# Experts stage: two buffers for the split activations, and VectorE and GpSimd exchange halves of the low second weights

## The chip, the cores and the metric

The kernel runs on one core of one Trainium2 chip. The metric is the device time of one execution in microseconds (us), given as the median of several runs. Five engines work side by side: TensorE (PE, whose weight loads the profile lists apart as PEld), VectorE (DVE), ScalarE (ACT), GpSimd (POOL) and SyncE (SP, which here only issues DMAs). They share the on-chip memory SBUF and wait for one another with semaphores. TensorE writes into PSUM.

## The reference, cut to what matters

The program is a chain of four blocks over 32 sequences of 112 rows of 256 features: cross attention, self attention with a mixture of experts behind it, a second cross attention, and a linear layer on quantised values. The change lies in the mixture of experts alone:

```python
gate_logits = nx @ gate_W
topk_vals, topk_idx = jax.lax.top_k(gate_logits, TOP_K)          # 2 of 8 experts
for e in range(N_EXPERTS):
    h = jax.nn.gelu(jnp.einsum('bsd,fd->bsf', nx, fc1_w[e]) + fc1_b[e], approximate=False)
    y = jnp.einsum('bsf,df->bsd', h, fc2_w[e]) + fc2_b[e]        # 1024 features -> 256
    moe_out = moe_out + y * dense_gates[..., e:e + 1]
```

## The kernel before

The rows that chose an expert lie in DRAM sorted by expert (`slots`), and `experts` works through them in 63 tiles of 128 rows (`MOE_TILES`), each of one expert. All second weights (`mem["w2"]`) lie in SBUF; the first weights of a tile (1 MB) come by DMA, two tiles ahead.

For a tile t there are two products. The first gives 1024 hidden features (`hidden`, L1428, 32 matmuls), to which ScalarE applies the Gelu (`act_T`, L1336, eight instructions). The second product, y, is made at the speed of rounded numbers (type fp32r) and with nearly the precision of float32: each operand is split into a rounded part and what the rounding left over, and three products are summed, high x high, high x low and low x high (L1447 and L1448, 8 chunks of 128 features, 3 matmuls each, 24 in all). Each split part has one buffer of its own, used by all tiles in turn:

- `w2H`, the rounded second weights, by ScalarE in two halves of 1024 elements (`weights_high`, L1328; counted by `w2_high`, two a tile). The first half belongs to the chunks 0 to 3, the second to 4 to 7.
- `aH`, the rounded activations, by ScalarE (L1343, `a_high`).
- `aL`, the low activations, `act_T` minus `aH`, by VectorE (L1399, `a_low`).
- `w2L`, the low second weights, `w2` minus `w2H`: the first half by GpSimd (L1359, `w2_low`), the second by VectorE (L1401, `w2_low_late`).

Every engine has its own instruction queue and runs the same loop (`over_tiles`). In step t:

- TensorE: the hidden product of tile t, the two transposes that prepare the rows of tile t + 1 (L1436), then y of tile t - 1. Before y it waits for `a_high`, `a_low` and `w2_low`; ahead of chunk 4 it also waits for `w2_low_late`. After chunk 3 it raises `y_half`, after chunk 7 `y_mm`.
- ScalarE: the Gelu of tile t; after `y_half` (y of tile t - 1 has read its first half) the first half of `w2H`; after `y_mm` (y of tile t - 1 is done) `aH` and then the second half of `w2H`.
- VectorE: the copies of the transposed rows of tile t + 1 (L1386), then y of tile t - 1 out of PSUM with its bias (L1394, after `y_mm`), a load of tile t's expert number into a register (L1397), `aL`, and the second half of `w2L`.
- GpSimd: a load of the expert number (L1357) and the first half of `w2L`, as soon as the first half of `w2H` is there. It has nothing else in this stage.

When the stage ends, the next stage's instructions stand behind it in each queue, GpSimd's casts and subtractions of `cross_last` (L1579 to L1599) among them.

Of the kernel before, what the change touches and what calls it, by code (L numbers as in the profile page):

```python
# [13 lines left out]
F32R = mybir.dt.float32r  # L14
BF16 = mybir.dt.bfloat16
U32 = mybir.dt.uint32
ALU = mybir.AluOpType
ACT = mybir.ActivationFunctionType
# [630 lines left out]
def self_attention(nc, mem, w, residual):  # L649
# [3 lines left out]
    with ExitStack() as ctx:  # L653
# [43 lines left out]
        tiles, ends, spare = sb("tiles", [1, NE]), sb("ends", [1, NE]), sb("spare", [1, NE])  # L697
        past, skipped = (wqkv[0:1, i, 0:(MOE_TILES + 1) * NE].rearrange("p (t e) -> p t e", e=NE) for i in range(2))
        tile_at = sb("tile_at", [1, MOE_TILES + 1])
        held, held_dve = sb("held", [1, 4]), sb("held_dve", [1, 2])  # L700
        weights_in, cleared, wo_in = sem("weights_in"), sem("cleared"), sem("wo_in")
        nT_mm, nT_ready = sem("nT_mm"), sem("nT_ready")
        q_mm, q_whole, q_ready, q_rounded = sem("q_mm"), sem("q_whole"), sem("q_ready"), sem("q_rounded")
# [526 lines left out]
def experts(nc, mem, w, residual):  # L1230


    with ExitStack() as ctx:
# [10 lines left out]
        wf, mx = sb("wf", [128, 2 * D]), {n: sb(f"mx_{n}", [128, 2 * D]) for n in ("t", "magic", "q", "d")}  # L1244
        mx.update((n, sb(f"mx_{n}", [128, 2 * D // MX])) for n in ("scale", "inv"))
        lent = lambda n, rows, size: nc.alloc_sbuf_tensor_at(f"e_{n}", [128, size * D], F32R, offset=mem["lent_at"] + rows * D * 4)
        w2H, w2L, aH, aL = lent("w2H", 0, 8), lent("w2L", 8, 8), lent("aH", 16, 4), lent("aL", 20, 4)
        w2_high, w2_low, w2_low_late, a_high, a_low, y_half = (sem(n) for n in ("w2_high", "w2_low", "w2_low_late", "a_high", "a_low", "y_half"))
        mx_step, w_ready = sem("mx_step"), sem("w_ready")
        NCH = HID // 128  # L1250
# [15 lines left out]
        def emit(block):  # L1266
# [53 lines left out]
            @block.scalar  # L1320
            def _(act):
                act.wait_ge(mem["fc1_b_in"], 16)
                act.wait_ge(mem["routed"], 1)
                act.wait_ge(mem["w2_in"], 16 * NE)
                act.wait_ge(mem["saved"], 16 * (NB - LENT))

                def weights_high(e, half):
                    act.activation(w2H[:, half * HALF:(half + 1) * HALF], weights_half(e, half), ACT.Copy).then_inc(w2_high, 1)  # L1328

                def step(t, par):  # L1330
                    if exists(t, MOE_TILES):
                        e = act.value_load(mem["tile_expert"][0:1, bass.ds(t, 1)], min_val=0, max_val=NE - 1)
                        act.wait_ge(h_mm, t + 1)
                        wait(act, a_low, t - 1)
                        for c in range(NCH):
                            last = act.activation(act_T[par][:, c * TILE:(c + 1) * TILE], hidden[par][:, c // 4, (c % 4) * TILE:(c % 4 + 1) * TILE],  # L1336
                                                  ACT.Gelu, bias=b1[:, bass.ds(e, 1), c:c + 1].rearrange("p a c -> p (a c)"))
                        last.then_inc(h_ready, 1)
                        wait(act, y_half, t)
                        weights_high(e, 0)  # L1340
                        act.wait_ge(h_ready, t + 1)
                        wait(act, y_mm, t)
                        act.activation(aH[:, :], act_T[par], ACT.Copy).then_inc(a_high, 1)  # L1343
                        weights_high(e, 1)
                    if isinstance(t, int) and t == 1:
                        mem["round_weights"](act)

                over_tiles(act, step)

            @block.gpsimd  # L1350
            def _(pool):
                pool.wait_ge(mem["routed"], 1)
                pool.wait_ge(mem["w2_in"], 16 * NE)

                def step(t, par):
                    if exists(t, MOE_TILES):
                        e = pool.value_load(mem["tile_expert"][0:1, bass.ds(t, 1)], min_val=0, max_val=NE - 1)  # L1357
                        pool.wait_ge(w2_high, 2 * t + 1)
                        pool.tensor_tensor(w2L[:, 0:HALF], weights_half(e, 0), w2H[:, 0:HALF], ALU.subtract).then_inc(w2_low, 1)  # L1359

                over_tiles(pool, step)

            @block.vector
            def _(dve):
# [12 lines left out]
                def step(t, par):  # L1377
# [18 lines left out]
                    if exists(t, MOE_TILES):  # L1396
                        e = dve.value_load(mem["tile_expert"][0:1, bass.ds(t, 1)], min_val=0, max_val=NE - 1)  # L1397
                        dve.wait_ge(a_high, t + 1)
                        dve.tensor_tensor(aL[:, :], act_T[par], aH[:, :], ALU.subtract).then_inc(a_low, 1)  # L1399
                        dve.wait_ge(w2_high, 2 * t + 2)  # L1400
                        dve.tensor_tensor(w2L[:, HALF:2 * HALF], weights_half(e, 1), w2H[:, HALF:2 * HALF], ALU.subtract).then_inc(w2_low_late, 1)  # L1401
                    if isinstance(t, int) and t == MOE_TILES - 1:
                        dve.wait_ge(bias_in, 32)
                        for action in quantise[:EARLY]:
# [9 lines left out]
            def _(pe):  # L1414
# [5 lines left out]
                def step(t, par):  # L1420
# [17 lines left out]
                    if exists(t - 1, MOE_TILES):  # L1438
# [4 lines left out]
                        for c in range(NCH):  # L1443
                            rows, cols = slice(c * TILE, (c + 1) * TILE), slice(c * D, (c + 1) * D)
                            if c == quarter:
                                pe.wait_ge(w2_low_late, t)
                            for i, (left, right) in enumerate(((aH, w2H), (aH, w2L), (aL, w2H))):  # L1447
                                last = pe.matmul(y_ps[:, 0:D], left[:, rows], right[:, cols], start=(c == 0 and i == 0), stop=(c == NCH - 1 and i == 2))  # L1448
                            if c == quarter - 1:
                                last.then_inc(y_half, 1)  # L1450
# [699 lines left out]
def program(nc, names, args, out):  # L2150
    w = dict(zip(names, args))
    ctx_t = w["ctx_t"]
    with ExitStack() as ctx:
# [18 lines left out]
        mem["saved"], mem["returned"] = sem("saved"), sem("returned")  # L2172
        mem["kept_rows"] = nc.dram_tensor("kept_rows", [T, NB - LENT, D], F32, kind="Internal").ap()
        mem["rates"], mem["shifts"], mem["rates_ready"] = sb("rates", [T, NB, 2]), sb("shifts", [T, NB, 2]), sem("rates_ready")
        first = cross_first(nc, mem, ctx_t, w, residual)
        with ExitStack() as weights:
            for name, shape in (("room", [128, ROOM]), ("w1", [128, 2, 2, HID]), ("w2", [128, NE, HID // 128, D])):
# [53 lines left out]
```

## Time and profile before

| | us |
|---|---|
| median of 3 runs (1979.08 to 1984.09) | 1982.87 |
| the profiled execution | 1980.91 |
| its span, first to last instruction | 1978.8 |
| the experts' y products, first to last start (trace) | 863.11 to 1290.37 |

Shares of the span: TensorE 95% busy, its weight loads 83%, VectorE 76%, ScalarE 64%, GpSimd 56%. TensorE's mean granted clock is 0.975 of full speed.

The page gives the busy time of each engine, the span in slices, the chain of work that ended last, and groups of instructions by line with what ended the idle time before them. Matmuls overlap, so a busy TensorE is not one at its peak; a weight load's row (PEld) shows by its start where a matmul began. A stage is read best from the timeline of each engine, in order of time.

### The profile page before, as it was taken

To read this page: it belongs to the slowest core of one execution; us is meant where nothing else is said; L and a number is where in the kernel's file an instruction comes from. 1 tells how busy PE (TensorE), PEld (TensorE's weight loads), DVE (VectorE), ACT (ScalarE), POOL (GpSimd) and SP (SyncE) were. 2 spreads that over 40 slices of the span, in tenths; PEclk is the share of its full clock that TensorE was granted. 3 is DMA by queue.
4 is the path that set the end of the run, shared out by engine and by line. 5 is a ranking of instruction groups with operands and counts; after the bars stand their busy time and mean duration, and the time that the engine had idled before them with its cause. 6 is when DMAs were issued, how large, how long until landed. Compare 5 with 4: busy or idle time off the path is not lost.

```text
span 1978.8 us, 61792 instructions
## 1 busy us (share of the span) xinstructions
PE 1877.6 (95%) x20887; PEld 1642.6 (83%) x20887; DVE 1498.3 (76%) x3375; ACT 1264.7 (64%) x2720; POOL 1098.7 (56%) x1680
## 2 busy tenths in 40 slices
PE   7999999999699999889999999959999999999996
PEld 5888888888578888689999999958888888888895
DVE  6788878877378888656666666666888888888886
ACT  2555555555377777557777777737767777777773
POOL 4565556555157676623333333377676767676751
PEclk9999999999799999899999999969999999999998
DMA  8222322331051111175555555421111111111100
GB/s 235 89 87 88 115 87 87 98 108 30 1 181 32 37 37 39 61 259 185 187 191 200 191 185 187 157 78 59 36 33 42 33 41 30 40 34 40 34 15 10
DMA packets 116596, 182.05 MB, mean 92 GB/s; under 512 B 10851, under 2 KB 94563, under 8 KB 116067
## 3 DMA queue, kind: packets, MB, share of 16 engines
q1 hardware_dynamic: 110386, 166.51, 26.2%
q0 software_dynamic: 6144, 14.69, 2.5%
q8 instruction: 40, 0.66, 0.1%
q14 instruction: 26, 0.21, 0.0%
HBM read 127.68 MB, written 53.48 MB: 92 GB/s over the span
## 4 chain that ended last, share of the span: by engine, by line
PE 52%; DVE 2%; issue 1%; POOL 1%; ACT 1%; DMA 0%; ACTq 0%; POOLq 0%; DVEq 0%
PE ps_quad L1428 11%; PE ps_out L1448 9%; PE ps_quad L182 6%; PE ps_quad L102 4%; PE ps_out L114 4%; PE ps_turned L108 4%; PE ps_quad L1879 3%; PE ps_proj L1899 3%; PE ps_turned L182 3%; PE ps_proj L182 2%; PE ps_proj L1904 1%; PE ps_proj L1436 1%; DVE c_negmax L119 1%; ACT c_probs L134 0%; PE ps_quad L1894 0%
## 5 line engine op out<-in xcount | busy, mean ns | idle before, releaser
L1359 POOL TENSOR_TENSOR e_w2L<-w,e_w2H 128x1024 fp32r<-128x1024 f32 x63 | 149.2, 2369 | 294.1 <-ACT e_w2H L1328 294.1
L1428 PE MATMUL ps_quad<-e_xT,w 128*128 128x128 f32 x2016 | 235.9, 275 | 1.7 <-DVE e_xT L1386 1.7
L1428 PEld LDWEIGHTS ps_quad<-e_xT,w 128*128 128x128 f32 x2016 | 231.1, 192 | 2.2 <-DVE e_xT L1386 2.2
L364 ACT ACTIVATE a_probsT<-ps_quad 125x1792 f32<-125x1792 f32 x96 | 159.8, 1665 | 101.6 <-PE ps_quad L533 101.6
L1336 ACT ACTIVATE e_act_T<-ps_quad,fc_b 128x128 f32<-128x128 f32 x504 | 137.0, 383 | 97.9 <-PE ps_quad L1428 97.7
L134 ACT ACTIVATE c_probs<-ps_quad,c_negmax 112x375 f32<-112x375 f32 x256 | 143.6, 571 | 66.2 <-DVE c_negmax L119 66.2
L1399 DVE TENSOR_TENSOR e_aL<-e_act_T,e_aH 128x1024 fp32r<-128x1024 f32 x63 | 151.8, 2409 | 37.9 <-ACT e_aH L1343 37.9
L1448 PE MATMUL ps_out<-e_w2H,e_aH 128*128 128x256 f32 x504 | 148.8, 295 | 13.3 <-DVE e_aL L1399 7.1
L126 DVE TENSOR_SCALAR c_probs<-c_probs,c_recip 112x375 f32<-112x375 f32 x256 | 150.9, 630 | 4.6
L421 DVE TENSOR_REDUCE a_negmax<-ps_turned 112x2 f32<-112x750 f32 x128 | 120.1, 938 | 34.1 <-PE ps_turned L519 33.9
L119 DVE TENSOR_REDUCE c_negmax<-ps_quad 112x2 f32<-112x750 f32 x128 | 114.0, 930 | 41.4 <-PE ps_quad L102 40.9
L1448 PE MATMUL ps_out<-e_w2H,e_aL 128*128 128x256 f32 x504 | 143.8, 285 | 0.0
L1448 PE MATMUL ps_out<-e_w2L,e_aH 128*128 128x256 f32 x504 | 143.7, 285 | 0.0
L419 DVE TENSOR_REDUCE a_negmax<-ps_quad 112x4 f32<-112x1500 f32 x64 | 110.2, 1721 | 36.5 <-PE ps_quad L519 36.5
L1328 ACT ACTIVATE e_w2H<-w 128x1024 fp32r x126 | 134.9, 1071 | 1.7 <-PE ps_out L1448 1.7
L1448 PEld LDWEIGHTS ps_out<-e_w2H,e_aH 128*128 128x128 f32 x504 | 97.3, 193 | 20.3 <-issue 18.9
L1394 DVE TENSOR_TENSOR e_y<-ps_out,e_b 128x256 f32<-128x256 f32 x63 | 26.8, 425 | 110.0 <-PE ps_out L1448 110.0
L108 PEld LDWEIGHTS ps_turned<-ident,c_probs 112*125 112x125 f32 x768 | 100.8, 188 | 7.6 <-issue 2.4
L108 PE MATMUL ps_turned<-ident,c_probs 112*125 112x112 f32 x768 | 103.8, 271 | 1.8 <-ACT c_probsT L130 1.8
L130 ACT ACTIVATE c_probsT<-ps_turned 125x672 f32<-125x672 f32 x128 | 95.1, 743 | 10.7 <-PE ps_turned L108 8.2
L359 ACT ACTIVATE a_kT<-ps_proj,a_bk 128x376 f32<-128x376 f32 x64 | 36.7, 574 | 101.0 <-PE ps_proj L182 101.0
L1448 PEld LDWEIGHTS ps_out<-e_w2H,e_aL 128*128 128x128 f32 x504 | 97.6, 194 | 0.0
(352 smaller groups left out, 6012.4 us busy)
## 6 DMA issues: line engine op xcount, KB each, us to landing
w<-in_fc_t SPq DMA_DIRECT2D x71, 1024.0 KB, 4.9
slots<-a_zeros SPq DMA_DIRECT2D x60, 512.0 KB, 4.9
a_cT<-in_ctx_t SPq DMA_DIRECT2D x32, 375.0 KB, 3.5
c_cT<-in_ctx_t SPq DMA_DIRECT2D x32, 375.0 KB, 3.2
e_xg<-slots SPq DMA_DIRECT2D x63, 128.0 KB, 3.9
slots<-e_y SPq DMA_DIRECT2D x63, 128.0 KB, 1.7
out<-c_fo SPq DMA_DIRECT2D x32, 112.0 KB, 1.9
residual<-in_x SPq DMA_DIRECT2D x1, 2912.0 KB, 19.0
```

The source lines that it names most:

```text
L108: last = pe.transpose(self.turned[:, j, c * T:(c + 1) * T], self.probs[u][:, j, c * self.chunk:(c + 1) * self.chunk], ident[0:T, 0:T])
L119: dve.tensor_reduce(self.negmax[:, u, :], self.scores[u % 2], AX, ALU.max, negate=True).then_inc(self.max_ready, 1)
L126: last = dve.tensor_scalar(p, p, self.recip[:, u, j:j + 1], None, ALU.mult)
L134: last = act.activation(self.probs[u][:, j, :], self.scores[u % 2][:, j, :], ACT.Exp, bias=self.negmax[:, u, j:j + 1], accum_out=self.sums ...
L182: last = pe.matmul(dst, left, right, start=(i == 0), stop=(i == len(terms) - 1))
L364: act.activation(probsT[:, 2 * i:2 * i + 2, :, :].rearrange("p c r x -> p r c x"), quad[0:KC, :, 0:2 * HALF].rearrange("p r (c x) -> p r c ...
L1328: act.activation(w2H[:, half * HALF:(half + 1) * HALF], weights_half(e, half), ACT.Copy).then_inc(w2_high, 1)
L1336: last = act.activation(act_T[par][:, c * TILE:(c + 1) * TILE], hidden[par][:, c // 4, (c % 4) * TILE:(c % 4 + 1) * TILE], ACT.Gelu, bias= ...
L1359: pool.tensor_tensor(w2L[:, 0:HALF], weights_half(e, 0), w2H[:, 0:HALF], ALU.subtract).then_inc(w2_low, 1)
L1399: dve.tensor_tensor(aL[:, :], act_T[par], aH[:, :], ALU.subtract).then_inc(a_low, 1)
L1428: last = pe.matmul(hidden[par][:, c // 4, (c % 4) * TILE:(c % 4 + 1) * TILE], mem["w1"][:, par, k, c * 128:(c + 1) * 128], xT[par][:, k, : ...
L1448: last = pe.matmul(y_ps[:, 0:D], left[:, rows], right[:, cols], start=(c == 0 and i == 0), stop=(c == NCH - 1 and i == 2))
```

## The change

`aH` and `aL` get a second buffer each, by the tile's parity. ScalarE rounds the activations right after the Gelu (it waits for its own `h_ready` and for y of tile t - 2), ahead of both halves of `w2H`, where the rounding stood between them and waited for y of tile t - 1. VectorE and GpSimd exchange the halves of `w2L`: VectorE makes the first half after `aL`, as soon as the first half of `w2H` is there; GpSimd makes the second, after the second half of `w2H`. The semaphores go with the halves: `w2_low` is now VectorE's, `w2_low_late` GpSimd's. Two small tiles (`held`, `held_dve`) are allocated in another place.

```diff
-        w2H, w2L, aH, aL = lent("w2H", 0, 8), lent("w2L", 8, 8), lent("aH", 16, 4), lent("aL", 20, 4)
+        w2H, w2L = lent("w2H", 0, 8), lent("w2L", 8, 8)
+        aH = [lent("aH0", 16, 4), ctx.enter_context(nc.sbuf_tensor("e_aH1", [128, HID], F32R))]
+        aL = [lent("aL0", 20, 4), ctx.enter_context(nc.sbuf_tensor("e_aL1", [128, HID], F32R))]
...
                         last.then_inc(h_ready, 1)
+                        act.wait_ge(h_ready, t + 1)
+                        wait(act, y_mm, t - 1)
+                        act.activation(aH[par][:, :], act_T[par], ACT.Copy).then_inc(a_high, 1)
                         wait(act, y_half, t)
                         weights_high(e, 0)
-                        act.wait_ge(h_ready, t + 1)
                         wait(act, y_mm, t)
-                        act.activation(aH[:, :], act_T[par], ACT.Copy).then_inc(a_high, 1)
                         weights_high(e, 1)
...
-                        pool.wait_ge(w2_high, 2 * t + 1)
-                        pool.tensor_tensor(w2L[:, 0:HALF], weights_half(e, 0), w2H[:, 0:HALF], ALU.subtract).then_inc(w2_low, 1)
+                        pool.wait_ge(w2_high, 2 * t + 2)
+                        pool.tensor_tensor(w2L[:, HALF:2 * HALF], weights_half(e, 1), w2H[:, HALF:2 * HALF], ALU.subtract).then_inc(w2_low_late, 1)
...
                         dve.wait_ge(a_high, t + 1)
-                        dve.tensor_tensor(aL[:, :], act_T[par], aH[:, :], ALU.subtract).then_inc(a_low, 1)
-                        dve.wait_ge(w2_high, 2 * t + 2)
-                        dve.tensor_tensor(w2L[:, HALF:2 * HALF], weights_half(e, 1), w2H[:, HALF:2 * HALF], ALU.subtract).then_inc(w2_low_late, 1)
+                        dve.tensor_tensor(aL[par][:, :], act_T[par], aH[par][:, :], ALU.subtract).then_inc(a_low, 1)
+                        dve.wait_ge(w2_high, 2 * t + 1)
+                        dve.tensor_tensor(w2L[:, 0:HALF], weights_half(e, 0), w2H[:, 0:HALF], ALU.subtract).then_inc(w2_low, 1)
...
-                            for i, (left, right) in enumerate(((aH, w2H), (aH, w2L), (aL, w2H))):
+                            for i, (left, right) in enumerate(((aH[1 - par], w2H), (aH[1 - par], w2L), (aL[1 - par], w2H))):
```

## Rows read from the trace of the kernel before

**Rows 1.** The page, busy us, share of the span, instructions.

```profile
PE 1877.6 (95%) x20887; PEld 1642.6 (83%) x20887; DVE 1498.3 (76%) x3375; ACT 1264.7 (64%) x2720; POOL 1098.7 (56%) x1680
```

**Rows 2.** Busy us per engine by stretch, then granted clock, DMA share, GB/s.

```profile
863.11:1290.37 427.26, 418.13 (x3560) 411.58 (x3560) 285.08 (x309) 315.61 (x679) 147.96 (x66) 1.00 0.56 191
```

**Rows 3.** Timeline, PEld: start us, us, instruction [idle before, releaser].

```profile
1043.21 0.19 PEld L1448 LDWEIGHTS ps_out<-e_w2H,e_aH 128*128 128x128 f32 x1 [0.38 <-issue]
...
1046.07 3.66 PEld L1428 LDWEIGHTS ps_quad<-e_xT,w 128*128 128x128 f32 x32
1049.65 0.25 PEld L1436 LDWEIGHTS ps_proj<-ident,e_xg 128*128 128x128 f32 x2
1049.87 0.19 PEld L1448 LDWEIGHTS ps_out<-e_w2H,e_aH 128*128 128x128 f32 x1
```

**Rows 4.** Timeline, GpSimd and VectorE in the same tile.

```profile
1046.28 2.38 POOL L1359 TENSOR_TENSOR e_w2L<-w,e_w2H 128x1024 fp32r<-128x1024 f32 x1 [4.22 <-ACT e_w2H L1328]
...
1046.60 0.42 DVE L1394 TENSOR_TENSOR e_y<-ps_out,e_b 128x256 f32<-128x256 f32 x1 [1.68 <-PE ps_out L1448]
1047.55 2.19 DVE L1399 TENSOR_TENSOR e_aL<-e_act_T,e_aH 128x1024 fp32r<-128x1024 f32 x1 [0.53 <-ACT e_aH L1343]
```

**Rows 5.** Lines L1399 and L1401, duration ns min/median/max of 63.

```profile
L1399 DVE TENSOR_TENSOR e_aL<-e_act_T,e_aH x63: 1224/2602/2652, 860.4 to 1287.7; 128x1024 fp32r<-128x1024 f32 x63
...
L1401 DVE TENSOR_TENSOR e_w2L<-w,e_w2H x63: 1210/1212/3333, 863.0 to 1290.2; 128x1024 fp32r<-128x1024 f32 x63
```

**Rows 6.** Timeline, ScalarE, one tile.

```profile
1042.98 2.17 ACT L1336 ACTIVATE e_act_T<-ps_quad,fc_b 128x128 f32<-128x128 f32 x8 [1.58 <-PE ps_quad L1428]
1045.04 1.06 ACT L1328 ACTIVATE e_w2H<-w 128x1024 fp32r x1
1046.45 1.06 ACT L1343 ACTIVATE e_aH<-e_act_T 128x1024 fp32r<-128x1024 f32 x1 [0.35 <-PE ps_out L1448]
1047.42 1.04 ACT L1328 ACTIVATE e_w2H<-w 128x1024 fp32r x1
```

**Rows 7.** Line L1397, VectorE's sequencer, duration ns min/median/max.

```profile
L1397 DVEq TENSOR_LOAD <-tile_expert x63: 300/308/544, 855.2 to 1286.6; - x63
```

**Rows 8.** Timeline, GpSimd and VectorE at the end of the stage.

```profile
1289.37 0.98 POOL L1579 TENSOR_TENSOR c_held<-minus_half 1x1 f32<-1x1 f32 x1
...
1291.20 1.28 POOL L1597 TENSOR_TENSOR c_wkL<-c_wk,c_wkH 128x512 fp32r<-128x512 f32 x1
1292.55 2.14 POOL L1599 TENSOR_TENSOR c_wkH<-c_wk,c_wkH 64x512 fp32r<-64x512 f32 x1
...
1287.67 2.63 DVE L1399 TENSOR_TENSOR e_aL<-e_act_T,e_aH 128x1024 fp32r<-128x1024 f32 x1 [0.64 <-ACT e_aH L1343]
1290.23 3.33 DVE L1401 TENSOR_TENSOR e_w2L<-w,e_w2H 128x1024 fp32r<-128x1024 f32 x1
```

**Rows 9.** Busy us per engine by stretch; the third number from the right is the clock.

```profile
861.10:863.10 2.00, 0.00 (x0) 0.00 (x0) 2.00 (x2) 2.00 (x9) 0.85 (x1) 1.00 0.75 240
863.10:864.50 1.40, 1.36 (x11) 1.39 (x12) 1.40 (x3) 0.27 (x2) 0.00 (x0) 1.00 1.00 367
864.50:867.90 3.40, 3.40 (x18) 3.40 (x17) 0.57 (x2) 1.36 (x2) 1.61 (x1) 0.50 1.04 392
...
499.30:506.10 6.80, 6.52 (x70) 4.87 (x70) 1.04 (x6) 2.35 (x4) 2.15 (x6) 0.50 0.00 0
...
1341.00:1345.00 4.00, 4.00 (x40) 3.64 (x42) 2.41 (x4) 3.25 (x8) 3.88 (x7) 1.00 0.17 23
```

**Rows 10.** Timeline, PEld and PE, where they had stalled.

```profile
863.11 0.19 PEld L1448 LDWEIGHTS ps_out<-e_w2H,e_aH 128*128 128x128 f32 x1 [3.37 <-issue]
867.08 4.07 PEld L1428 LDWEIGHTS ps_quad<-e_xT,w 128*128 128x128 f32 x32
...
498.82 0.41 PE L548 MATMUL ps_turned<-ident,a_negmax 112*128 112x112 f32 x2 [1.21 <-DVE a_negmax L419]
...
1340.92 0.33 PE L1879 MATMUL ps_quad<-c_xT,c_wq 128*128 128x112 f32 x1 [1.00 <-ACT c_probs L134]
```

More of the change, by code:

```diff
@@ L699, in self_attention @@
         tile_at = sb("tile_at", [1, MOE_TILES + 1])
-        held, held_dve = sb("held", [1, 4]), sb("held_dve", [1, 2])
+        held, held_dve = mem["held"], mem["held_dve"]
         weights_in, cleared, wo_in = sem("weights_in"), sem("cleared"), sem("wo_in")
@@ L2174, in program @@
         mem["rates"], mem["shifts"], mem["rates_ready"] = sb("rates", [T, NB, 2]), sb("shifts", [T, NB, 2]), sem("rates_ready")
+        mem["held"], mem["held_dve"] = sb("held", [1, 4]), sb("held_dve", [1, 2])
         first = cross_first(nc, mem, ctx_t, w, residual)
```

## The prediction

> **What bounds the kernel now.** I read the page's shares first: TensorE is busy 95% of the span and no other engine over 76% [rows 1]. Only the experts stage is touched, so the next view is the stretch from the first start of the y products to the last: 427.26 us, TensorE busy 418.13, clock 1.00 [rows 2]. Those are 62 periods of 6.89 us. The timeline of weight loads shows a period's parts: y from 1043.21 to 1046.07 is 2.86, the hidden product and two transposes up to the next y at 1049.87 are 3.80, together 6.66 [rows 3]. What is over, 0.38, is an idle wait in front of y, in every second tile. All the change can give is thus 62 x (6.89 - 6.66) = 14 us.
>
> What ends that wait? VectorE's aL. It takes 1.22 at the least, but 2.60 in the median [rows 5]. The timeline says why: GpSimd's subtraction runs from 1046.28 to 1048.66, aL is issued at 1047.55 and ends at 1049.74, 1.08 after GpSimd has ended [rows 4]. It does nearly all its work after GpSimd, whenever it was issued. So two subtractions on these two engines, both from SBUF to SBUF, do not run side by side here. VectorE's copy of y out of PSUM, issued inside the same GpSimd instruction, took its 0.42 [rows 4]; it isn't held.
>
> At the end of the stage the same thing is seen the other way round [rows 8]. GpSimd's one-element operation, issued at 1289.37, ends at 1290.35, just after aL (1290.30). VectorE's second half of w2L was issued at 1290.23, seven hundredths before aL ended. Yet GpSimd goes first, and the half takes 3.33, to 1293.56, that is 1.09 after GpSimd's subtraction of 1291.20 to 1292.48. The next GpSimd subtraction, issued at 1292.55, ends at 1294.69, 1.13 after VectorE: it waited, and only some 0.15 of the 1.28 that the one before it took was hidden in that wait. So each engine waits for the other's whole instruction, and a waiting GpSimd goes before the next VectorE instruction, even one that follows at once.
>
> The Trainium skill's page "SBUF — State Buffer", section "SBUF: two separate sides", states such a rule: VectorE instructions with two SBUF inputs and GpSimd's share a port pair, which the first to start holds for its whole instruction while the other is fully blocked. If the held GpSimd subtraction then ran its whole 2.37, and not 0.14 less as the row has it, each period below would be 0.14 longer, 9 us in all. The trace agrees with the lock and puts the hidden start-up at 0.15.
>
> **The change, part by part.** Times are from the first weight load of y of tile t - 1, for a tile without idle time. ScalarE: the Gelu starts at 0.15 (1042.98 is 0.23 ahead of 1043.21, less the idle 0.38) and ends at 2.3 [rows 3, 6]. aH follows at 2.35, where it stood at 3.24; the new buffer is what allows it, since y of tile t - 2 is long done. Consecutive copies start 0.97 apart [rows 6]: w2H's first half at 3.3 to 4.4, its second at 4.3 to 5.35 (it may not start before 3.24). ScalarE's work is the same, done before the next Gelu at 6.8. GpSimd, 0.18 behind the copy it waits for (1046.10 to 1046.28), is issued at 5.5, where it was issued at 3.07.
>
> VectorE: it must first copy y out, at 3.39 (1046.60 - 1043.21). Then comes the register load of 0.31 with its bookkeeping [rows 7]. No row shows how soon aL could follow, since aH always came later; it lies between 0.42 (the copy's own time) and 0.95 (1046.60 to 1047.55) [rows 4]. I take 0.8, since the load and three more sequencer steps have to pass. aL then runs at 4.2 to 5.4 unhindered (1.22), and w2L's first half at 5.35 to 6.55 (1.21) [rows 5]. y of tile t could start at 6.66: this half is just in time.
>
> But VectorE now holds the memory from 4.2 to 6.55, and GpSimd asks at 5.5. It runs from 6.55 and ends at 6.55 + 2.37 - 0.14 = 8.8. TensorE needs the second half four chunks into y, at 6.66 + 1.43 = 8.1. It stalls 0.7 in the middle of y. That stall delays the end of y, hence VectorE's copy and aL by 0.7 (aL at 4.9 to 6.1 of the next tile), but not GpSimd's request: it still comes at 5.5, now inside aL. By rows 8 GpSimd then goes before the first half of w2L, for which TensorE waits at the start of y.
>
> From there the order keeps itself. Counted from the end of a y product (E): copy at 0.53, aL 1.33 to 2.55. ScalarE waited for the same end and runs w2H's second half at 0.38 to 1.42 [rows 6]; GpSimd asks at 1.60, inside aL again. GpSimd 2.55 to 4.78, w2L's first half until 4.78 + 1.08 = 5.86, y at 5.94. TensorE was ready at 3.80, so it idles 2.14 in front of every y. The period is 2.86 + 5.94 = 8.8 in place of 6.89: 62 x 1.91 = 118 us. If aL came 0.3 later, GpSimd would go ahead of it and the period would be 9.1; if 0.3 earlier, 8.5. So +99 to +137 before the clock.
>
> **The clock.** Stalls of 3.37 and of 1.21 were each followed by a fall of the granted clock from 1.00 to 0.50 (2.4 to 1.2 GHz); after one of 1.00 it stayed [rows 9, 10]. A stall of 2.14 lies between two that fell, so I take it to fall. At 863 it fell 1.4 after TensorE had resumed, at 498.8 it fell 0.5 after, and the first low stretch lasted 3.4 us: y then took 867.08 - 863.11 = 3.97, 1.11 more than 2.86 [rows 10]. Had that stretch lain wholly in y, y would have lost up to half of it, some 1.5. The price per tile lies between 0 and 1.5; I take 1.4, as a shorter stall lets the fall come sooner, like the one at 498.8. A slow stretch under the hidden product costs nothing, since 2.14 of slack cover it. 62 x 1.4 = 87 us.
>
> Sum: 118 + 87 = 205, on the profiled execution's 1980.9 (span 1978.8; the median of 1982.87 is 0.1% above it): 2186 us.
>
> At nothing I cost: the moved small tiles; SyncE's DMAs, as none is moved and a longer period leaves them more time; VectorE's copy of the transposed rows, now queued behind the late half, which ends 0.1 before y starts and so leaves it y's 2.86 for its 0.72. Behind GpSimd's later wait nothing of this stage is queued. Behind ScalarE's new wait stand the two copies, but it is met. The first and last tile may add or take 3 us; not counted.
>
> **Rivals.**
> 1. The same order, but the clock stays at 1.00: 1980.9 + 118 = 2099. For it: the stall of 1.00 without a fall. Against it: a fall after 1.21.
> 2. VectorE keeps the memory for both of its instructions whenever GpSimd's request falls into aL. Then only the stall in the middle of y is left, 0.7 to 0.8 a tile: period 7.4, 62 x 0.5 = 32, 2013 us. Against it: the same pair of instructions at 1290.23 let GpSimd in between.
> 3. The other side, faster: GpSimd's second half meets its date. It is in time if it ends by 8.1, so if it gets the memory by 5.9; that needs VectorE's two subtractions to be over by then, 0.65 earlier than I have it, or not to hold GpSimd's at all. From that point on TensorE's period is 6.66: minus 14 us, 1967. For it: rows 4 show this pair with only VectorE waiting; no row has a 128x1024 GpSimd subtraction held. Against it: 1292.55 in rows 8, which was.
>
> **How the numbers follow.** Forecast 0.63 (own range 2160 to 2210), rival 1 0.18, rival 2 0.05, rival 3 0.09, no change 0.03, slower in another way 0.02. The range must take in the forecast and rival 1 with the bounds of aL's start (2099 - 19 = 2080): 2080 to 2210, which leaves out 0.19. A measurement tells this kernel from no change at about 0.3%, 6 us: faster 0.09, same 0.03, slower 0.88.
>
> **What would show it.** In the profile after: aL at about 1.22 in nearly all tiles; VectorE's half of w2L at 3.3, in place of 1.21; GpSimd's subtraction at some 3.2 (0.95 of waiting), in place of 2.37; TensorE idle some 2.1 in front of y with VectorE's w2L as what ended it; a clock well under 1.00 from 870 to 1290. aL still long with GpSimd's unhindered at 2.37 would be wrong order; a period of 7.4 with the idle time in front of chunk 4 would be rival 2; GpSimd and VectorE side by side at 2.37 and 1.21 with no idle TensorE, rival 3.

## The result and the profile after

The changed kernel takes 2183.61 us in the median of four runs (2176.62 to 2184.95), against 1983.48 for the kernel before: ratio 1.1012 (95% interval 1.0991 to 1.1032). It is 10% slower. The profiled execution took 2182.3 us, with a span of 2180.2. Where executions of an experiment came with a mean clock of 0.65 to 0.84 (four in all, of experiments 7 and 8), they are left out of its ratio and its bounds.

The page, busy us and shares of the span, and the chain of work that ended last. They answer to [rows 1]: TensorE is listed as more busy than before, 1962.5 in place of 1877.6, with the same 20887 instructions, so its instructions have become longer. VectorE's subtraction of `w2L` is now 10% of the chain.

```profile
PE 1962.5 (90%) x20887; PEld 1721.2 (79%) x20887; DVE 1558.0 (71%) x3375; ACT 1283.7 (59%) x2720; POOL 1145.0 (53%) x1680
...
PE ps_out L1451 12%; DVE e_w2L L1404 10%; PE ps_quad L182 6%; PE ps_quad L102 4%; PE ps_out L114 3%; PE ps_turned L108 3%; PE ps_quad L1882 3%; PE ps_turned L182 3%; PE ps_proj L1902 3%; PE ps_proj L182 2%; ACT e_w2H L1330 2%; PE ps_proj L1907 1%; DVEq L1400 1%; DVE c_negmax L119 1%; ACT c_probs L134 0%
```

Busy time by stretch, from the first start of the y products to the last, in the columns of [rows 2]. Then one y product that ran at full clock, and the next, which did not.

```profile
865.32:1495.40 630.08, 500.94 (x3560) 487.89 (x3560) 347.14 (x309) 334.17 (x683) 196.40 (x67) 0.86 0.38 130
1045.56:1048.41 2.85, 2.82 (x23) 2.85 (x24) 0.42 (x2) 2.16 (x3) 0.00 (x0) 1.00 0.90 355
...
1054.45:1058.46 4.01, 3.98 (x23) 4.01 (x24) 0.41 (x2) 2.32 (x3) 0.00 (x0) 0.65 0.66 263
```

The stretch is 630.08 in place of 427.26, 202.8 more; the span grew by 201.4. So the whole loss lies here. A period is 630.08 / 62 = 10.16 in place of 6.89, and the clock is 0.86 in place of 1.00.

Instructions that write `aL` and `w2L`, duration ns min/median/max, as in [rows 5].

```profile
L1402 DVE TENSOR_TENSOR e_aL<-e_act_T,e_aH x63: 1224/1225/1227, 862.8 to 1490.7; 128x1024 fp32r<-128x1024 f32 x63
...
L1404 DVE TENSOR_TENSOR e_w2L<-w,e_w2H x63: 1218/3400/3424, 864.0 to 1491.8; 128x1024 fp32r<-128x1024 f32 x63
L1362 POOL TENSOR_TENSOR e_w2L<-w,e_w2H x63: 2565/3112/3191, 864.9 to 1491.2; 128x1024 fp32r<-128x1024 f32 x63
```

`aL`, which had been held (2602 in the median), now never is. VectorE's half of `w2L`, which had been free (1212), is held in nearly every tile, and GpSimd's subtraction has 0.75 of waiting in it (3112 against 2367 before).

Timelines of ScalarE, GpSimd, VectorE and the weight loads, one tile, to be read beside [rows 3, 4, 6].

```profile
1048.82 1.06 ACT L1330 ACTIVATE e_w2H<-w 128x1024 fp32r x1 [0.37 <-PE ps_out L1451]
...
1050.06 3.08 POOL L1362 TENSOR_TENSOR e_w2L<-w,e_w2H 128x1024 fp32r<-128x1024 f32 x1 [5.80 <-ACT e_w2H L1330]
...
1048.94 0.42 DVE L1397 TENSOR_TENSOR e_y<-ps_out,e_b 128x256 f32<-128x256 f32 x1 [2.96 <-PE ps_out L1451]
1049.69 1.22 DVE L1402 TENSOR_TENSOR e_aL<-e_act_T,e_aH 128x1024 fp32r<-128x1024 f32 x1 [0.33 <-issue]
1050.83 3.39 DVE L1404 TENSOR_TENSOR e_w2L<-w,e_w2H 128x1024 fp32r<-128x1024 f32 x1
...
1045.56 0.19 PEld L1451 LDWEIGHTS ps_out<-e_w2H,e_aH 128*128 128x128 f32 x1 [2.27 <-issue]
1048.41 3.66 PEld L1431 LDWEIGHTS ps_quad<-e_xT,w 128*128 128x128 f32 x32
1051.99 0.25 PEld L1439 LDWEIGHTS ps_proj<-ident,e_xg 128*128 128x128 f32 x2
1054.45 0.19 PEld L1451 LDWEIGHTS ps_out<-e_w2H,e_aH 128*128 128x128 f32 x1 [2.21 <-issue]
```

Read it from the end of y, 1048.41. GpSimd asks 1.65 later, in the middle of `aL` (1049.69 to 1050.91), and is let in when `aL` ends, although VectorE's half is issued at 1050.83. GpSimd ends at 1053.14, VectorE's half 1.08 after that, at 1054.22, and y starts 0.23 later. TensorE, ready at 1052.24, has idled 2.21.

The first three y products, weight loads:

```profile
865.32 0.19 PEld L1451 LDWEIGHTS ps_out<-e_w2H,e_aH 128*128 128x128 f32 x1 [2.33 <-issue]
867.52 0.19 PEld L1451 LDWEIGHTS ps_out<-e_w2H,e_aH 128*128 128x128 f32 x1 [0.71 <-POOL e_w2L L1362]
...
874.80 0.19 PEld L1451 LDWEIGHTS ps_out<-e_w2H,e_aH 128*128 128x128 f32 x1 [2.03 <-issue]
```

The first y stalls 0.71 ahead of chunk 4, on GpSimd. That delays its end, and from the second y on the stall is in front of y and about 2 us long.

### The profile page after: what moved, and what is told of

Read it like the earlier page. It is cut to its first block, busy times and chain, and to the rows that moved or that the text cites. A ratio compares the mean times of both kernels' runs of the same rounds, so it can differ in the third digit from the quotient of the medians.

```text
span 2180.2 us, 61791 instructions
## 1 busy us (share of the span) xinstructions
PE 1962.5 (90%) x20887; PEld 1721.2 (79%) x20887; DVE 1558.0 (71%) x3375; ACT 1283.7 (59%) x2720; POOL 1145.0 (53%) x1680
## 4 chain that ended last, share of the span: by engine, by line
PE 40%; DVE 11%; issue 5%; ACT 2%; DVEq 1%; POOL 1%; ACTq 0%; DMA 0%; POOLq 0%
PE ps_out L1451 12%; DVE e_w2L L1404 10%; PE ps_quad L182 6%; PE ps_quad L102 4%; PE ps_out L114 3%; PE ps_turned L108 3%; PE ps_quad L1882 3%; PE ps_turned L182 3%; PE ps_proj L1902 3%; PE ps_proj L182 2%; ACT e_w2H L1330 2%; PE ps_proj L1907 1%; DVEq L1400 1%; DVE c_negmax L119 1%; ACT c_probs L134 0%
## 5 line engine op out<-in xcount | busy, mean ns | idle before, releaser
L1362 POOL TENSOR_TENSOR e_w2L<-w,e_w2H 128x1024 fp32r<-128x1024 f32 x63 | 195.6, 3105 | 449.5 <-ACT e_w2H L1330 449.5
L1451 PE MATMUL ps_out<-e_w2H,e_aH 128*128 128x256 f32 x504 | 183.1, 363 | 131.3 <-DVE e_w2L L1404 130.8
L1451 PEld LDWEIGHTS ps_out<-e_w2H,e_aH 128*128 128x128 f32 x504 | 132.1, 262 | 144.5 <-issue 143.8
L1397 DVE TENSOR_TENSOR e_y<-ps_out,e_b 128x256 f32<-128x256 f32 x63 | 26.7, 425 | 263.4 <-PE ps_out L1451 263.4
L1404 DVE TENSOR_TENSOR e_w2L<-w,e_w2H 128x1024 fp32r<-128x1024 f32 x63 | 212.0, 3366 | 0.0
L1451 PE MATMUL ps_out<-e_w2H,e_aL 128*128 128x256 f32 x504 | 178.9, 355 | 0.0
L1451 PE MATMUL ps_out<-e_w2L,e_aH 128*128 128x256 f32 x504 | 178.4, 354 | 0.0
L1451 PEld LDWEIGHTS ps_out<-e_w2H,e_aL 128*128 128x128 f32 x504 | 134.1, 266 | 0.0
L1451 PEld LDWEIGHTS ps_out<-e_w2L,e_aH 128*128 128x128 f32 x504 | 133.7, 265 | 0.0
```

The source lines that it names most:

```text
L1362: pool.tensor_tensor(w2L[:, HALF:2 * HALF], weights_half(e, 1), w2H[:, HALF:2 * HALF], ALU.subtract).then_inc(w2_low_late, 1)
L1404: dve.tensor_tensor(w2L[:, 0:HALF], weights_half(e, 0), w2H[:, 0:HALF], ALU.subtract).then_inc(w2_low, 1)
```

## The experiments

**Theory.** Two subtractions on VectorE and GpSimd, both with all their inputs in SBUF, exclude each other for whole instructions (the lock). The time goes to the order in which the two engines get it (about 120 us), and to the clock, which falls after the stalls this order makes (about 85 us). **Rivals.** The lock is no part of it, and VectorE or GpSimd simply has too much to do; the second buffers, not the exchange, cost the time; the clock would have fallen anyway.

**1. No GpSimd: VectorE makes both halves.**

```diff
-                        pool.tensor_tensor(w2L[:, HALF:2 * HALF], ...).then_inc(w2_low_late, 1)
+                        dve.wait_ge(w2_high, 2 * t + 2)
+                        dve.tensor_tensor(w2L[:, HALF:2 * HALF], ...).then_inc(w2_low_late, 1)
```

> Both halves of the low second weights on VectorE (first half, then second half right behind it), GpSimd does nothing in the experts stage; the two buffers stay. Theory (VectorE's and GpSimd's subtractions hold the memory against each other for whole instructions): with GpSimd silent no subtraction on VectorE takes more than 1.22; counted from the start of a y product aL ends at 5.4, the first half at 6.55, the second at 7.7, and TensorE needs them at 6.66 and 8.1; period 6.66 to 6.7, clock 1.00, 1980.9 - 14 = 1967 us (1962 to 1971), faster than both kernels. Rival (it is the early rounding with its new order on VectorE, or simply too much low work late in the tile, that stalls TensorE): VectorE has 1.21 more to do in each tile, and the kernel stays at 2184 or gets slower.

Measured: 1974.88 us, ratio 0.9963 (0.995 to 0.9976). Taking work away from GpSimd and giving all of it to VectorE makes the changed kernel 209 us faster: VectorE doesn't have too much to do. (That GpSimd doesn't either, experiment 2 shows.) The gain over the kernel before is 8 us, less than expected, and only 0.4 of it lies between the first and the last y product (426.83 in place of 427.26); the rest lies ahead of them and behind. VectorE's timeline, GpSimd's and the weight loads show why:

```profile
895.03 1.57 DVE L1400 TENSOR_TENSOR e_aL<-e_act_T,e_aH 128x1024 fp32r<-128x1024 f32 x1 [0.34 <-issue]
896.52 2.29 DVE L1402 TENSOR_TENSOR e_w2L<-w,e_w2H 128x1024 fp32r<-128x1024 f32 x1
...
895.49 2.25 POOL L1600 TENSOR_TENSOR c_wkL<-c_wk,c_wkH 128x512 fp32r<-128x512 f32 x1
...
1047.61 1.22 DVE L1400 TENSOR_TENSOR e_aL<-e_act_T,e_aH 128x1024 fp32r<-128x1024 f32 x1 [0.32 <-issue]
...
1054.51 1.22 DVE L1400 TENSOR_TENSOR e_aL<-e_act_T,e_aH 128x1024 fp32r<-128x1024 f32 x1 [0.54 <-issue]
1055.65 1.22 DVE L1402 TENSOR_TENSOR e_w2L<-w,e_w2H 128x1024 fp32r<-128x1024 f32 x1
...
1057.09 0.19 PEld L1451 LDWEIGHTS ps_out<-e_w2H,e_aH 128*128 128x128 f32 x1 [0.24 <-issue]
```

In every second tile VectorE waits 0.54 and not 0.32 ahead of `aL`, its first half ends at 1056.87, and y follows 0.22 later, after 0.24 of idle time. And GpSimd isn't silent: with nothing left to do in this stage it makes the next stage's subtractions already from 895 on, and the lock stretches three of VectorE's halves to 2.3, with idle times of 1.46 and 1.32 in front of y.

**2. GpSimd is made to wait for VectorE's half.**

```diff
+                        pool.wait_ge(w2_low, t + 1)
                         pool.wait_ge(w2_high, 2 * t + 2)
```

> The changed kernel with one wait more: GpSimd starts its half only when VectorE's half of the same tile is done. Nothing is taken away. Theory (the loss comes from the order GpSimd before VectorE's second subtraction): VectorE's half falls from 3.38 to 1.21 and y starts without idle time; GpSimd runs 2.37 from 6.65 to 9.0 and TensorE stalls 0.9 in front of chunk 4, which needs it at 8.1; period 7.4 to 7.6, and as a stall of 1.00 did not lower the clock before, the clock stays near 1.00: 1980.9 + 62 x 0.6 = 2018 us (2010 to 2030). Rival (GpSimd's lateness alone is the cause): the wait makes GpSimd later still, so 2184 us or more.

Measured: 2037.73 us, ratio 1.0276 (1.0259 to 1.0294). The instructions that write `w2L`, and the weight load of chunk 4:

```profile
L1405 DVE TENSOR_TENSOR e_w2L<-w,e_w2H x63: 1215/1218/1221, 864.7 to 1348.3; 128x1024 fp32r<-128x1024 f32 x63
L1363 POOL TENSOR_TENSOR e_w2L<-w,e_w2H x63: 2386/2397/2415, 866.2 to 1349.7; 128x1024 fp32r<-128x1024 f32 x63
...
1047.87 0.19 PEld L1452 LDWEIGHTS ps_out<-e_w2H,e_aH 128*128 128x128 f32 x1 [1.01 <-POOL e_w2L L1363]
```

The same work on the same engines in the other order, with one wait more, is 146 us faster. Both subtractions run at their free length, and the stall has moved in front of chunk 4 and is 1.01; the period is 7.80 and the clock of the stretch 1.00. The order was the cause, not the amount.

**3. VectorE's half reads its first input from PSUM.**

```diff
-  dve.tensor_tensor(w2L[:, 0:HALF], weights_half(e, 0), w2H[:, 0:HALF], ALU.subtract)
+  dve.tensor_tensor(w2L[:, 0:HALF], hidden[par].rearrange("p a f -> p (a f)"), w2H[:, 0:HALF], ALU.subtract)
```

> The changed kernel, but VectorE's half of the low second weights takes its first input from PSUM (the tile's hidden features, the same 128x1024 float32) where it took the weights from SBUF; so the low first half is not the weights' remainder, and the output is not the reference's. Same engines, sizes, order and waits. Theory (what is held is the memory access of a VectorE instruction with two SBUF inputs): this instruction takes about 1.2 also while GpSimd runs; GpSimd, asking at 5.5 after aL's end at 5.4, takes 2.37 and is done at 7.9, before 8.1; period 6.7, no idle time, about 1967 us (1960 to 1975). Rival (the two engines keep each other from running whatever the memory, or share it by bandwidth): still 3.4 for the half, 2184 us.

Measured: 1972.5 us, ratio 0.9953 (0.9938 to 0.9969). The same two lines:

```profile
L1404 DVE TENSOR_TENSOR e_w2L<-ps_quad,e_w2H x63: 1214/1217/1219, 858.8 to 1277.5; 128x1024 fp32r<-128x1024 f32 x63
L1362 POOL TENSOR_TENSOR e_w2L<-w,e_w2H x63: 2383/2409/3119, 859.8 to 1277.9; 128x1024 fp32r<-128x1024 f32 x63
```

With GpSimd's operation, its place and its waits as in the changed kernel, one input of VectorE's taken from elsewhere gives back all of the 200 us and 11 more. Near 1042 the half is issued at 1042.32 and GpSimd's subtraction at 1042.46, and both run at their free length side by side. So the exclusion needs both of VectorE's inputs in SBUF. The Trainium skill's page "SBUF — State Buffer", section "SBUF: two separate sides", names a VectorE operation with two SBUF inputs as one that takes the pair of ports shared with GpSimd. The run agrees: with one input in PSUM, 1.217 beside 2.409. The half made here isn't that of the weights, so this run prices the lock and is no remedy.

**4. The stall is filled.** Eleven transposes whose result nobody reads stand before each y on TensorE; no other engine waits for them.

```diff
+                    if exists(t - 1, MOE_TILES):
+                        for i in range(FILL):          # FILL = 11
+                            pe.transpose(psum["turned"][:, 0, 0:128], ident[:, :], ident[:, :])
```

> The changed kernel with 11 transposes of the identity into an unused PSUM area ahead of each y product, about 11 x 0.164 = 1.8 us of TensorE work in the 2.0 us in which it idles. Theory (1.4 of the 3.3 us per tile are the granted clock, which falls after each stall): the clock stays at 1.00 and y takes 2.86, the waits behind VectorE's half stay; period 8.8, 2099 us (2090 to 2112), 85 us less than the changed kernel although TensorE does more. Rival (y is long for another reason, such as the memory's other readers): y stays at 4.0 to 4.3 and the time at 2184 us or more.

Measured: 2105.34 us, ratio 1.0617 (1.0599 to 1.0634). Stretch of the y products, and a y's first weight load:

```profile
860.29:1415.38 555.09, 496.18 (x4242) 483.00 (x4242) 349.08 (x309) 334.16 (x683) 198.83 (x67) 1.00 0.43 147
...
1048.70 0.19 PEld L1455 LDWEIGHTS ps_out<-e_w2H,e_aH 128*128 128x128 f32 x1 [1.04 <-issue]
```

TensorE has 682 instructions more in this stretch, and the kernel is 78 us faster: the idle time is cut to 1.04 (the eleven take 1.2 us, not the 1.8 reckoned) and the clock stays at 1.00. The period is 555.09 / 62 = 8.95. So the loss of the changed kernel splits into (8.95 - 6.89) x 62 = 128 us for the order and (10.16 - 8.95) x 62 = 75 us for the clock. The changed kernel's own periods at full clock, 8.89 from 1045.56 to 1054.45, give nearly the same split, 124 and 79.

**5. The buffers alone, halves as before; 6. the exchange alone, single buffers.**

```diff
 # 5: the changed kernel, but
+                        pool.tensor_tensor(w2L[:, 0:HALF], ...).then_inc(w2_low, 1)
+                        dve.tensor_tensor(w2L[:, HALF:2 * HALF], ...).then_inc(w2_low_late, 1)
 # 6: the kernel before, but
+                        pool.tensor_tensor(w2L[:, HALF:2 * HALF], ...).then_inc(w2_low_late, 1)
+                        dve.tensor_tensor(w2L[:, 0:HALF], ...).then_inc(w2_low, 1)
```

> Only the second buffers of the change: GpSimd keeps the first half of w2L and VectorE the second, as before. Theory (the lock, and a waiting GpSimd goes before VectorE's next instruction): the early aH moves w2H's first half to 3.3 to 4.4 after the start of y, so GpSimd asks at about 4.55, inside aL (4.2 to 5.4); it runs until some 7.65 and y starts about 1.0 late; VectorE's half after it is in time for chunk 4. After a late y, ScalarE is ahead, GpSimd asks at about 3.2 and the next y starts nearly on time, so the stalls alternate. Mean period 7.0 to 7.7 in place of 6.89: 1990 to 2035 us, slower than before, with the idle time in front of y ended by GpSimd. Rival (the exchange of the halves alone costs the time, buffers are harmless or help): 1965 to 1985 us. Second rival (the buffers cost all of it): 2150 us or more.

> Only the exchange of the halves: VectorE the first, GpSimd the second, with single buffers as before, so aH starts after the end of y. Counted from that end: aH 0.38 to 1.4, w2H's second half 1.35 to 2.4, GpSimd asks at 2.6; aL 1.47 to 2.69. Theory with GpSimd asking inside aL, by less than 0.1 us: GpSimd runs first, until 4.95, VectorE's half until 6.0, y starts at 6.1, TensorE idle 2.3 in front of y, period 8.96 and a falling clock: 2100 to 2210 us, as the whole change. Rival, aL ends before GpSimd asks: VectorE's half goes first, is over at 3.9, y starts nearly on time and the stall is in front of chunk 4, about 0.8 us with a period of 7.6 to 7.8: 2020 to 2040 us, like the kernel in which GpSimd was made to wait. Second rival (the exchange is harmless without the buffers): 1983 us.

Measured: the buffers alone 2011.1 us, ratio 1.0137 (1.0113 to 1.0162); the exchange alone 2188.65 us, ratio 1.1042 (1.1024 to 1.1061). The exchange by itself costs all of it; the buffers cost 30 us by themselves, in the alternation that was expected. GpSimd and the starts of y with the buffers alone:

```profile
1041.68 3.23 POOL L1362 TENSOR_TENSOR e_w2L<-w,e_w2H 128x1024 fp32r<-128x1024 f32 x1 [5.56 <-ACT e_w2H L1330]
1048.46 2.39 POOL L1362 TENSOR_TENSOR e_w2L<-w,e_w2H 128x1024 fp32r<-128x1024 f32 x1 [3.56 <-ACT e_w2H L1330]
...
1045.13 0.19 PEld L1451 LDWEIGHTS ps_out<-e_w2H,e_aH 128*128 128x128 f32 x1 [1.21 <-issue]
1052.01 0.19 PEld L1451 LDWEIGHTS ps_out<-e_w2H,e_aH 128*128 128x128 f32 x1 [0.19 <-issue]
```

With the exchange alone, VectorE and GpSimd:

```profile
1044.12 1.23 DVE L1399 TENSOR_TENSOR e_aL<-e_act_T,e_aH 128x1024 fp32r<-128x1024 f32 x1 [0.52 <-ACT e_aH L1343]
1045.27 3.38 DVE L1401 TENSOR_TENSOR e_w2L<-w,e_w2H 128x1024 fp32r<-128x1024 f32 x1
...
1045.22 2.35 POOL L1359 TENSOR_TENSOR e_w2L<-w,e_w2H 128x1024 fp32r<-128x1024 f32 x1 [8.22 <-ACT e_w2H L1328]
```

GpSimd asks at 1045.22, 0.13 before `aL` ends and 0.05 before VectorE's half is issued, and that is enough in all 63 tiles: VectorE's half takes 3.37 to 3.40 in each.

**7. Single buffers, all on VectorE; 8. two buffers, all on VectorE, and an early register load.** The first is the kernel before without GpSimd's half. The second is experiment 1 with:

```diff
+                        if exists(t, MOE_TILES):
+                            own = dve.value_load(mem["tile_expert"][0:1, bass.ds(t, 1)], ...)
                         dve.wait_ge(y_mm, t)
...
-                        e = dve.value_load(mem["tile_expert"][0:1, bass.ds(t, 1)], ...)
+                        e = own
                         dve.wait_ge(a_high, t + 1)
```

> The kernel before with GpSimd's half of w2L moved to VectorE, single buffers kept. Theory (what the kernel before loses in front of y is aL held by GpSimd; the buffers are worth next to nothing): aL 4.33 to 5.55 after the start of y, first half until 6.7, y at 6.75 to 6.8 in place of 6.66, second half until 7.85 against a need at 8.1. Period 6.75 to 6.8: 62 x 0.09 to 0.14 = 6 to 9 us less than before, 1974 to 1978 us, within 3 us of the kernel with all on VectorE and two buffers. Rival (the second buffers are what gains): 1983 us or more.

> The kernel with two buffers and all of w2L on VectorE, and VectorE's register load for the next tile ahead of the copy of y. In that kernel y waits 0.24 us in every second tile for VectorE's first half; aL follows the copy's start by 0.75 in one tile and 0.96 in the next. Theory (the load and its bookkeeping stand on the path): aL comes 0.33 to 0.54 earlier, the wait is gone, period 6.66 to 6.7, 62 x 0.12 = 7 us less than the 1974.9 us of that kernel: 1964 to 1970 us, faster than before by 0.6 to 1%. Rival (the wait is not VectorE's chain): 1975 us.

Measured: with single buffers 1985.9 us, ratio 1.0008 (0.9997 to 1.0018), no gain; with the early load 1965.35 to 1968.41 us, ratio 0.9919 (0.9902 to 0.9936). The first expectation was wrong by 8 to 12 us. VectorE's half and the weight load behind it, with single buffers:

```profile
1050.86 1.22 DVE L1399 TENSOR_TENSOR e_w2L<-w,e_w2H 128x1024 fp32r<-128x1024 f32 x1
...
1052.30 0.19 PEld L1448 LDWEIGHTS ps_out<-e_w2H,e_aH 128*128 128x128 f32 x1 [0.23 <-issue]
```

`aL` started where it was expected, 1.48 after the end of y, but y starts 0.22 after VectorE's half has ended, where 0.05 to 0.1 had been reckoned, and that in nearly every tile: period 6.92. The next stage's work on GpSimd, which experiment 1 showed, holds VectorE here too and costs some 3 us more. So with all on VectorE the two buffers are worth up to 11 us (1985.9 - 1974.9; the two profiled executions differ by 5.4), and the load 9 more.

**9. The changed kernel with the early load, twice.** The same edit as in 8, on the changed kernel; GpSimd keeps its half.

> The changed kernel, with VectorE's register load for the next tile moved ahead of the copy of y, so that aL follows the copy after about 0.42 us in place of 0.75 to 0.83. The prediction said that an aL that comes 0.3 earlier shortens the period by as much and leaves the order. Theory: the order keeps itself (GpSimd still asks inside aL), the period falls by 0.33 to 0.4 us, 62 times that is 20 to 25 us: about 2160 us if the clock falls as before, down to 2085 us if a stall of 1.8 us no longer lowers it. Rival: the order breaks, since aL is now over before GpSimd asks; then VectorE's half goes first and the stall in front of chunk 4 is left, 2010 to 2040 us. Second rival (the period is not set by VectorE's chain): 2183 us.

> The changed kernel with the early load once more, since it took 2077 to 2079 us in three executions and 1988 us in one at the same granted clock. Theory (two orders that keep themselves; which one a run falls into is settled by the first tiles): each execution is near 2077 or near 1988 us, none between; in the short one GpSimd's subtraction runs 2.4 and VectorE's half 1.22 in most tiles, in the long one 2.70 and 3.43. Rival (a disturbance of that one run): all near 2077 us, or scattered.

Measured: of 13 executions ten took 2076.8 to 2081.2 us and three 1982.3 to 1988.0, none between, all at a mean clock of 0.975 to 0.980. A profile of each, first of a long one, then of a short one (VectorE, GpSimd, weight loads):

```profile
1046.56 1.22 DVE L1404 TENSOR_TENSOR e_aL<-e_act_T,e_aH 128x1024 fp32r<-128x1024 f32 x1
1047.69 3.44 DVE L1406 TENSOR_TENSOR e_w2L<-w,e_w2H 128x1024 fp32r<-128x1024 f32 x1
...
1047.33 2.71 POOL L1362 TENSOR_TENSOR e_w2L<-w,e_w2H 128x1024 fp32r<-128x1024 f32 x1 [5.77 <-ACT e_w2H L1330]
...
1051.35 0.19 PEld L1453 LDWEIGHTS ps_out<-e_w2H,e_aH 128*128 128x128 f32 x1 [1.84 <-issue]
```

```profile
1045.54 1.22 DVE L1404 TENSOR_TENSOR e_aL<-e_act_T,e_aH 128x1024 fp32r<-128x1024 f32 x1
1046.67 1.22 DVE L1406 TENSOR_TENSOR e_w2L<-w,e_w2H 128x1024 fp32r<-128x1024 f32 x1
...
1047.13 3.04 POOL L1362 TENSOR_TENSOR e_w2L<-w,e_w2H 128x1024 fp32r<-128x1024 f32 x1 [3.91 <-ACT e_w2H L1330]
...
1050.22 0.19 PEld L1453 LDWEIGHTS ps_out<-e_w2H,e_aH 128*128 128x128 f32 x1 [0.27 <-POOL e_w2L L1362]
```

One program, two orders, and each keeps itself. In the long one y ends at 1045.69 and GpSimd asks 1.64 later, inside `aL`. In the short one y ends at 1044.67 and GpSimd asks 2.46 later, when `aL` is over and VectorE's half has begun; what is left is 0.27 ahead of chunk 4. ScalarE explains the two dates: where y starts late, its Gelu is long done and it waits only for the end of y; where y is on time, it still has the Gelu and two copies to do. What seems to have sent the profiled short run into its order is a row of ScalarE in the second tile, first of the short run, then of the long one, where the data were there:

```profile
872.42 1.06 ACT L1534 ACTIVATE c_wkH<-c_wk 128x1024 fp32r<-128x1024 f32 x1 [1.65 <-DMA c_wk<-in_L_xattn_Wk]
...
875.06 2.17 ACT L1338 ACTIVATE e_act_T<-ps_quad,fc_b 128x128 f32<-128x128 f32 x8 [0.24 <-issue]
```

```profile
868.69 1.04 ACT L1534 ACTIVATE c_wkH<-c_wk 128x1024 fp32r<-128x1024 f32 x1
```

The Gelu starts 5.76 after the end of the first y (869.30), in the long run 4.06 (867.32 to 871.38). A DMA that came late once kept ScalarE, hence GpSimd's next request, behind `aL`, and the order stayed for the 60 tiles left. This is read from one pair of traces, which also differ in the clock of the first y; no run delays that DMA alone. That it must be late enough, the changed kernel's trace suggests: there ScalarE waits 1.28 for the same data, in place of 1.65, and GpSimd's request (879.65) still falls inside `aL` (878.86 to 880.09). That the other short executions began in the same way isn't shown; they have no profile. The long order has one more thing to tell: its stalls of 1.84 leave the clock of the stage at 0.99 to 1.00, where those of 2.0 to 2.4 in the changed kernel go with 0.86, so the 0.4 to 0.5 us that `aL` comes earlier are worth 106 us.

**10. The kernel before with the Gelu's result in PSUM; 11. the same in the changed kernel.** The Gelu writes back into the `hidden` tile that it reads, and `aH` and `aL` take it from there.

```diff
-  last = act.activation(act_T[par][:, c * TILE:(c + 1) * TILE], hidden[par][:, c // 4, ...], ACT.Gelu, ...)
+  last = act.activation(hidden[par][:, c // 4, ...], hidden[par][:, c // 4, ...], ACT.Gelu, ...)
-  dve.tensor_tensor(aL[:, :], act_T[par], aH[:, :], ALU.subtract).then_inc(a_low, 1)
+  dve.tensor_tensor(aL[:, :], hidden[par].rearrange("p a f -> p (a f)"), aH[:, :], ALU.subtract).then_inc(a_low, 1)
```

> The kernel before, except that the Gelu writes its result back into the PSUM tile that it reads, and aH and aL take it from there. Theory (an instruction of VectorE with one input in PSUM is not held by GpSimd): aL takes 1.22 beside GpSimd's subtraction of 2.4, from about 4.35 to 5.6 after the start of y, and y starts at 6.66 without the 0.38 of idle time in every second tile: 1965 to 1972 us. Rival (the lock holds VectorE whatever its input): aL 2.6 as before, 1980 to 1986 us. Should the Gelu or the copy take longer on PSUM, ScalarE has about 1 us of slack in 6.66.

> The changed kernel, with the Gelu's result kept in PSUM, so that aL no longer shares anything with GpSimd. Theory: that does not save the change, since VectorE's first half is still held. Counted from the end of y: GpSimd asks at 1.65 and runs at once, until 4.0; aL runs beside it, 1.3 to 2.5; VectorE's half is issued at 2.45 and ends 1.1 after GpSimd, at 5.1; y starts at 5.2. TensorE idles 1.4 in front of y, period 8.06 in place of 6.89: 62 x 1.17 = 73 us more than before, 2056 us if a stall of 1.4 leaves the clock as the 1.84 of the kernel with the early load did; up to 2120 us if it falls. Rival (aL's place in the lock was the cause): GpSimd and VectorE's half meet their dates, 1963 to 1985 us.

Measured: on the kernel before 1963.43 us (1961.35 to 1963.52), ratio 0.9896 (0.9881 to 0.991), the fastest of all; on the changed kernel 2058.32 us, ratio 1.0392 (1.037 to 1.0414), where 2056 was reckoned. The first one's stretch of y products, GpSimd and VectorE:

```profile
861.11:1273.97 412.86, 409.60 (x3560) 409.08 (x3561) 234.23 (x309) 312.41 (x682) 147.34 (x65) 1.00 0.58 198
...
1045.02 2.37 POOL L1359 TENSOR_TENSOR e_w2L<-w,e_w2H 128x1024 fp32r<-128x1024 f32 x1 [4.36 <-ACT e_w2H L1328]
...
1045.79 1.23 DVE L1399 TENSOR_TENSOR e_aL<-ps_quad,e_aH 128x1024 fp32r<-128x1024 f32 x1 [0.52 <-ACT e_aH L1343]
```

`aL` runs inside GpSimd's subtraction at its free length, and the period is 412.86 / 62 = 6.66, TensorE's own. In the second, `aL` is free too, but VectorE's half isn't:

```profile
1051.17 2.39 POOL L1362 TENSOR_TENSOR e_w2L<-w,e_w2H 128x1024 fp32r<-128x1024 f32 x1 [5.81 <-ACT e_w2H L1330]
...
1051.94 2.69 DVE L1404 TENSOR_TENSOR e_w2L<-w,e_w2H 128x1024 fp32r<-128x1024 f32 x1
...
1054.86 0.19 PEld L1451 LDWEIGHTS ps_out<-e_w2H,e_aH 128*128 128x128 f32 x1 [1.51 <-issue]
```

The half that y starts with, and GpSimd asking before it: that still costs 78 us against the kernel before. But `aL` counts too. GpSimd no longer waits for it, the stall is 1.51 in place of 2.2 and leaves the clock at 1.00, and so 125 of the 200 us come back.

## Why the prediction was right, point by point

The forecast was 2186 us; 2183.6 was measured.

- **What bounds the kernel before.** Right: the idle time in front of y was `aL` held by GpSimd. With `aL` out of the lock the kernel is at 6.66 a tile and 20 us faster (experiment 10). The stretch gives 427.26 - 412.86 = 14.4 of that, the 14 that the prediction had; in the two profiled executions 2.0 more lies ahead of it and 1.0 behind.
- **The lock and who goes first.** Right on both for this kernel (experiments 2, 3 and 11). In [rows 8] GpSimd had asked 0.86 before VectorE's half was issued (1289.37 and 1290.23); at experiment 6 a lead of 0.05 was enough. A general rule isn't shown: in [rows 8] the subtraction that GpSimd issued at 1291.20 also went before that half, which had waited since 1290.23, while in experiment 1 `aL`, waiting since 895.03, went before a GpSimd subtraction issued at 895.49. What decides there is open.
- **The first tile, 0.7 in the middle of y, then the order that keeps itself.** Right to the row: 0.71 at the first y, 2.03 in front of the second. The dates within a tile, from the end of y: copy 0.53 as reckoned; `aL` 1.28 (1.33); GpSimd asks 1.65 (1.60) and ends 4.73 (4.78); VectorE's half ends 5.81 (5.86); y starts 6.04 (5.94). The value chosen for the interval from the copy to `aL`, 0.8 between bounds of 0.42 and 0.95, was 0.75 and 0.83.
- **The order's price.** 118 us against 124 to 128 (experiment 4). TensorE mostly idles 2.2 to 2.3 in front of y, not 2.14: y starts 0.23 after VectorE's half has ended, and the prediction allowed 0.08. That is what y takes behind the end of `aL` in the kernel before (`aL` from 1040.49, 2.64 long, y at 1043.21); behind `w2L` it is longer. It is the same 0.22 that spoilt the expectation of experiment 7.
- **That an `aL` 0.3 earlier gives a period of 8.5.** Right in kind for the long order of experiment 9, which has 528.19 / 62 = 8.52, though there `aL` came 0.4 to 0.5 earlier and the period fell from 8.9, not 8.8; and only while the order lasts; that the same edit lets another order stand, 90 us faster, was not seen. It is close to rival 2, with a stall of 0.27 in place of 0.7.
- **The clock's price.** 87 us against 75 to 79. A period with a fallen clock is 10.2 to 10.5, one without 8.9, so a fall costs about 1.45 (1.4 was taken). But it fell in 52 of the 62 periods; four of the first five y products and then about every ninth ran at full clock, like the one at 1045.56. The two misses, 6 to 10 too little for the order and 8 to 12 too much for the clock, cancel: part of the forecast's closeness is luck. And the ground for letting the clock fall at all was weak. The prediction placed 2.14 between two stalls that were followed by a fall, 1.21 and 3.37; yet recurring stalls of 1.51 (experiment 11) and 1.84 (experiment 9), which lie between them too, left the clock alone. That 2.1 to 2.3 mostly was enough is thus luck as well; the chance of 0.18 for rival 1 covered it.
- **The rivals.** The clock that stays is experiment 4's state, 2105 us (2099 was worked out); GpSimd in time is experiment 3's, 1972.5 (1967); neither was the case here.

## What to carry to other kernels

Where two engines exclude each other, look at which of them is already asking when the lock comes free: here that, and not the amount of work, set the order. Then ask whether a stall that the order makes moves the requests so that it comes back in the next tile. Leave the instruction that the bound engine waits for without a competitor (experiment 1, 209 us in the changed kernel), or take one of its inputs from PSUM where it lies there anyway (experiment 10, 20 us in the kernel before). And price a recurring stall twice, by its length and by the granted clock; the second price keeps a chance of being nothing, since a single stall elsewhere in the trace didn't tell what a recurring one does.

## What the runs showed of the hardware that was not expected

- Recurring stalls of 1.51 (experiment 11) and 1.84 us (experiment 9) left the granted clock at 0.99 to 1.00 over the stretch. With stalls of 2.0 to 2.4 in the changed kernel it fell in 52 tiles of 62, and with those of 2.4 in experiment 6 in 48 of 62 (0.87 over the stretch); the other y products ran at full clock after stalls just as long. So the length of the stall alone doesn't decide; what else does is open.
- One program can have two lasting speeds, 1985 and 2078 us, at the same clock. In the one short execution that has a profile, a DMA that was late once came ahead of the change of order.
- TensorE's first weight load of y follows the end of the `w2L` half that it waits for by 0.22 to 0.23 us in nearly every tile (the changed kernel, experiments 1, 6 and 7), but the end of `aL` by 0.07 to 0.08 in most tiles of the kernel before in which TensorE waited. What makes the difference isn't known.
